# Softmax weights turned in 32x32 blocks on VectorE and multiplied by the values in sixteen 32x32 tiles, in a decoder layer in float32 on one core of Trainium2

## The chip, the cores and the metric

The kernel runs on one core of one Trainium2 chip. Its time is the device time of one execution in microseconds (us). Before the change it is 1048.2 us, the median of three runs (1045.29 to 1048.98). The engines are TensorE (PE in the profile, with its weight loads as PEld), VectorE (DVE), ScalarE (ACT), GpSimd (POOL) and SyncE (SP), which here only issues transfers.

## The reference: what is computed

One decoder layer with post-normalisation over x of 2 x 2048 rows of 512, all in float32: linear self-attention without softmax, cross-attention with 16 heads of 32 over 154 context rows, and a feed-forward part with token shift. Each ends in a residual sum and a layernorm.

```python
def _L0_xattn_ref(Query, Key, Values, Mask, ...):
    q = _split_heads(Query @ W_q.T + b_q)          # 16 heads of 32
    k = _split_heads(Key @ W_k.T + b_k)
    v = _split_heads(Values @ W_v.T + b_v)
    scores = jnp.einsum('bhqd,bhkd->bhqk', q, k) / jnp.sqrt(jnp.float32(D_K))
    scores = jnp.where(Mask == 0, jnp.float32(NEG_INF), scores)
    attn = jax.nn.softmax(scores, axis=-1)
    out = jnp.einsum('bhqk,bhkd->bhqd', attn, v)
    ...
    return out @ W_o.T + b_o
x = _layernorm(x + _L0_attn_ref(x, ...), axis=-1)
x = _layernorm(x + _L0_xattn_ref(x, ctx_1024, ctx_1024, mask, ...), axis=-1)
x = _layernorm(x + _L0_ffn_ref(x, ...), axis=-1)     # r = sigmoid(xr W_r), k = relu(xk W_k)^2, out = r * (k W_v)
```

## The kernel before, in words

There are three stages. `context_and_gram` (up to 97 us) loads x once and builds its Gram matrix, the keys and the values of the context. `fold` (to 188 us) folds the linear self-attention of each of the two batches into one matrix `m` and one row `c_row`. `layers` (the rest) runs the layer itself on 16 groups of 256 rows (two tiles of 128 rows, `t` = 0 and 1), 8 groups for each batch.

`layers` is a software pipeline that is written out by hand. The loop variable `n` is the group whose softmax runs; in the same pass group `a = n + 1` gets its self-attention product `y`, its layernorm, its turning (`x1_turn`) and its `q`; group `f = n - 1` gets the output product `o`, the second layernorm (`x2_turn`) and the mixing; group `e = n - 2` gets the products `k`, `r` and `v` of the feed-forward part. Each engine has its own program with its own order, and counts semaphores: `x.at(n, k)` is the count after k steps of group n. An engine runs its instructions in the order written, so a waiting instruction holds all behind it.

Each dense product is three float32r passes (`three_pass`, lines 81 to 83) over a high and a low part. Twelve such half products of 12 or 24 matmuls belong to one pass of the loop. They share two banks of PSUM, `d0` and `d1`.

The softmax of a group goes in four head groups `g` of 4 heads (32 partitions each in `q` and `kt`). For each: `scores` puts 8 products (2 tiles by 4 heads, 154 keys) into four banks; `masked_min` on VectorE adds the mask and takes the minimum of the negated scores, one instruction for each head; `exponentials` on ScalarE; `weigh` on GpSimd divides by the sum. The weights are then turned on TensorE (`transposes`): four 128x128 blocks for each tile (the first 128 keys), which ScalarE copies out (`take_turned`), and one block for each tile with the last 26 keys of the four heads, from a buffer of its own, `prob_rest` (`take_rest`). `values` multiplies: one 128x128 product for the 26 last keys of all heads and four 128x32 products for the first 128. `o_high` (ScalarE) and `o_low` (VectorE) split the result for the product `o`. A matmul on float32 data that is no transpose stands as two rows in the trace.

The names that the change and the prediction touch: `scores`, `transposes`, `values`, `masked_min`, `o_low`, `k_square`, `k_mix_low` (line 805), `v_finish` (lines 823 and 826, then `moments`), `normalise` (line 735), `weigh` (928 to 934).

## Time and profile before

| | |
|---|---|
| median of three runs | 1048.2 us (1045.29 to 1048.98) |
| the profiled execution | 1045.77 us, its span 1043.8 us |
| TensorE busy | 969.0 us, 6354 matmul rows and as many weight loads |
| VectorE busy | 648.7 us |
| ScalarE, GpSimd busy | 530.6 us, 527.3 us |
| one steady pass of the loop | 49.04 us |

The span is what the trace covers; the profiled execution took 2.0 us more than it. Busy time is a union of an engine's instructions, so a TensorE that reads 93% may still be waiting for nothing or be slowed within its rows: how far apart the starts of two rows are says more than their length. The steady pass is read from the first score row of one pass (602.58) to that of the next (651.62); the five passes from 553.55 to 798.73 are alike, at 49.03 to 49.04 us each.

### The profile page before, as it was taken

How to read it: one execution, taken by the hardware profiler on the slowest of the kernel's cores; microseconds unless marked ns; L12 is line 12 of the kernel's file. 1: busy time of each engine (PE TensorE's matmuls, PEld its weight loads, DVE VectorE, ACT ScalarE, POOL GpSimd, SP SyncE). 2: the span in 40 equal slices, each digit the busy share in tenths (PEclk: the TensorE clock that was granted, in tenths of full speed). 3: DMA queues.
4: the chain of work that ended last, by engine and by line, in shares of the span. 5: the costliest groups of instructions: out<-in, count | busy, mean ns of one | idle time of the engine just before them, and what ended most of it. 6: DMA issues, size and time to landing. Idle time of an engine off the chain costs nothing.

```text
span 1043.8 us, 18201 instructions
## 1 busy us (share of the span) xinstructions
PE 969.0 (93%) x6354; PEld 761.7 (73%) x6354; DVE 648.7 (62%) x1942; ACT 530.6 (51%) x1619; POOL 527.3 (51%) x525
## 2 busy tenths in 40 slices
PE   5999999667889999999999999999999999999875
PEld 4698474455677878878787878787877878787764
DVE  1243232245656867777778767777777677776753
ACT  1232022067565665656665656575756656565421
POOL 4283000147564756556657556474757566556310
PEclk9999999877989999999999999999999999999989
DMA  5253900100000101010110000000101010000001
GB/s 195 61 181 107 309 23 10 63 21 27 7 22 7 42 7 42 7 42 27 40 58 22 27 22 27 27 21 27 36 13 42 7 42 13 36 1 22 21 1 40
DMA packets 30853, 45.59 MB, mean 44 GB/s; under 512 B 2731, under 2 KB 15531, under 8 KB 30507
## 3 DMA queue, kind: packets, MB, share of 16 engines
q1 hardware_dynamic: 28363, 40.39, 11.9%
q10 hardware_dynamic: 2400, 4.05, 1.1%
q8 instruction: 51, 0.84, 0.3%
q14 instruction: 39, 0.32, 0.1%
HBM read 34.10 MB, written 9.70 MB: 42 GB/s over the span
## 4 chain that ended last, share of the span: by engine, by line
PE 66%; DVE 7%; issue 4%; ACT 3%; POOL 2%; DMA 1%; POOLq 0%; DVEq 0%
PE dense L81 18%; PE dense L83 16%; PE dense L82 16%; PE turned L1049 5%; PE scores L1039 3%; PE rest_value L1065 3%; PE rest_value L1062 3%; DVE mix_r_raw L799 2%; PE dense L999 1%; PE rest_value L1055 1%; DVE xt_lo L750 1%; ACT x_t L626 1%; ACT prob L584 1%; DVE prob L759 1%; DMA mask_in<-mask 1%
## 5 line engine op out<-in xcount | busy, mean ns | idle before, releaser
L928 POOL TENSOR_TENSOR row_inv<-row_sum,minus_one 128x4 f32<-128x4 f32 x128 | 143.1, 1118 | 187.8 <-ACT prob L584 187.8
L584 ACT ACTIVATE prob<-prob,row_min 128x154 f32<-128x154 f32 x512 | 209.8, 417 | 24.6 <-DVE row_min L759 24.5
L759 DVE CUSTOM_DVE_ANT_0 prob<-scores,mask_add 128x154 f32<-128x154 f32 x512 | 129.2, 310 | 44.2 <-PE scores L1039 44.2
L934 POOL TENSOR_TENSOR prob<-prob,row_inv 128x512 f32<-128x512 f32 x128 | 138.3, 1080 | 0.0
L592 ACT ACTIVATE prob_t<-turned 128x512 f32<-128x512 f32 x128 | 76.0, 594 | 102.9 <-PE turned L1049 102.9
L584 ACT ACTIVATION_READ_ACCUMULATOR prob<-prob,row_min 128x1 f32 x512 | 98.7, 193 | 0.0
L1049 PE MATMUL turned<-ident,prob 128*128 128x128 f32 x512 | 81.9, 284 | 8.5 <-POOL prob L934 4.6
L939 POOL TENSOR_TENSOR mix_r_lo<-mix_r_raw,mix_r_hi 128x1024 fp32r<-128x1024 f32 x16 | 38.2, 2390 | 100.3 <-ACT mix_r_hi L630 100.3
L81 PE MATMUL dense<-xt_hi,cross_wq_hi 128*128 128x256 f32 x256 | 78.2, 306 | 3.9 <-DVE xt_lo L750 3.9
L81 PE MATMUL dense<-mix_k_hi,ffn_wk_hi 128*128 128x256 f32 x256 | 74.3, 290 | 6.1 <-DVE xt_lo L750 4.4
L1049 PEld LDWEIGHTS turned<-ident,prob 128*128 128x128 f32 x512 | 60.0, 144 | 24.4 <-issue 10.7
L82 PE MATMUL dense<-xt_lo,cross_wq_hi 128*128 128x256 f32 x256 | 75.1, 293 | 0.0
L83 PE MATMUL dense<-xt_hi,cross_wq_lo 128*128 128x256 f32 x256 | 74.9, 293 | 0.0
L83 PE MATMUL dense<-mix_k_hi,ffn_wk_lo 128*128 128x256 f32 x256 | 71.4, 279 | 0.0
L82 PE MATMUL dense<-mix_k_lo,ffn_wk_hi 128*128 128x256 f32 x256 | 71.4, 279 | 0.0
L920 POOL TENSOR_TENSOR rstd<-var,neg_half 128x2 f32<-128x2 f32 x48 | 33.5, 698 | 74.2 <-DVE var L729 71.4
L173 POOL TENSOR_TENSOR x_sum<-x_sum,x_rows 128x512 f32<-128x512 f32 x32 | 48.0, 1500 | 36.6 <-DMA x_rows<-x_rows 32.6
L766 DVE TENSOR_TENSOR o_t_lo<-rest_value,o_t_hi 128x256 fp32r<-128x256 f32 x64 | 26.8, 419 | 62.2 <-ACT o_t_hi L603 62.2
L81 PE MATMUL dense<-ffn_wv_hi,k_act_hi 128*128 128x512 f32 x128 | 54.3, 424 | 8.3 <-DVE k_act_lo L817 8.3
L81 PEld LDWEIGHTS dense<-xt_hi,cross_wq_hi 128*128 128x128 f32 x256 | 51.8, 202 | 11.0 <-issue 6.2
L81 PEld LDWEIGHTS dense<-mix_k_hi,ffn_wk_hi 128*128 128x128 f32 x256 | 48.1, 188 | 15.5 <-issue 15.4
L81 PE MATMUL dense<-ffn_wr_hi,mix_r_hi 128*128 128x512 f32 x128 | 53.3, 416 | 3.8 <-ACT x_t L626 3.8
(143 smaller groups left out, 2653.0 us busy)
## 6 DMA issues: line engine op xcount, KB each, us to landing
x_rows<-x_rows SPq DMA_DIRECT2D x32, 256.0 KB, 2.8
xt_raw<-x_cols SPq DMA_DIRECT2D x16, 512.0 KB, 3.6
out<-gate_then_y SPq DMA_DIRECT2D x16, 512.0 KB, 2.8
mask_in<-mask SPq DMA_DIRECT2D x16, 154.0 KB, 2.3
w_v_raw<-cross_wv ACTq DMA_DIRECT2D x1, 1024.0 KB, 8.1
w_k_raw<-cross_wk ACTq DMA_DIRECT2D x1, 1024.0 KB, 10.8
self_wv<-self_wv ACTq DMA_DIRECT2D x1, 1024.0 KB, 5.2
self_wk<-self_wk SPq DMA_DIRECT2D x1, 1024.0 KB, 5.7
```

The source lines that it names most:

```text
L81: pe.matmul(out, sta[0], mov[0], start=first, stop=False, skip_group_check=True)
L82: pe.matmul(out, sta[0], mov[1], start=False, stop=False, skip_group_check=True)
L83: return pe.matmul(out, sta[1], mov[0], start=False, stop=last, skip_group_check=True)
L173: pool.tensor_tensor(x_sum[:, b, :], x_sum[:, b, :], x_in[t][:], ALU.add).then_inc(*summed.up)
L584: m = act.activation(keys, keys, ACT.Exp, bias=row_min[:, buf, t, h:h + 1], scale=-1.0, accum_out=row_sum[:, buf, t, h:h + 1])
L592: act.activation(pt[:, 0:HPG, t * P:(t + 1) * P], t_bank[:].rearrange("p (c n) -> p c n", c=HPG), ACT.Copy).then_inc(*t_out.up)
L759: m = dve.tensor_tensor_reduce(prob[buf][:, t, h * CTX:(h + 1) * CTX], s_bank[:, h, t * CTX:(t + 1) * CTX], mask_add[n % 2][:, t, :], -SCA ...
L920: pool.tensor_tensor(rs[:], var[:], neg_half[:], ALU.pow).then_inc(*ln_rstd[key].up)
L928: pool.tensor_tensor(row_inv[:, buf, t, :], row_sum[:, buf, t, :], minus_one[:], ALU.pow).then_inc(*p_inv.up)
L934: pool.tensor_tensor(keys[:, :, 0:P], keys[:, :, 0:P], inv.broadcast_to([P, HPG, P]), ALU.mult).then_inc(*p_norm.up)
L939: pool.tensor_tensor(mix["r"][1][:], mixed["r"][:], f32(mix["r"][0][:]), ALU.subtract).then_inc(*mix_lo["r"].up)
L1049: m = pe.transpose(t_bank[:, h * P:(h + 1) * P], prob[g % 2][:, t, h * CTX:h * CTX + P], ident[:])
```

## The change

Turning moves from TensorE to VectorE. For each tile and head group one instruction turns 640 columns (4 heads of 160, that is 154 keys padded to 5 blocks of 32) in blocks of 32x32, from `prob` into `prob_t`. In such a block the 32 keys lie on partitions, but each quarter of the partitions holds other rows of x, so `values` becomes 80 products of 32x32 stationary by 64 moving columns: 5 key blocks, 4 quarters of the partitions `i`, 4 heads. Quarter `i` writes to bank `i` of the four score banks, behind the scores. The values lie in SBUF four times over (`v_blocks`), are parked in DRAM and loaded for each batch (`load_values`). `transposes`, `take_turned`, `take_rest` and `prob_rest` are gone, and their two banks become dense banks: four in place of two, with other waits for a free bank. `scores` now waits until `o_low` has read the value part of the same banks (`ot_lo`), and `values` until `masked_min` has read the next scores (`s_min`). Two pieces move from VectorE to ScalarE: the layernorm's scaling (`normalise`, with a shift that GpSimd makes) and the square of the relu. Orders change with it: VectorE's `k_mix_low` now stands behind the minimum of the next group's first scores.

```diff
+def load_values(sp, v_blocks, v_park, b, flag):
+    first = v_park[b * CTX:b * CTX + 4 * DK, :].rearrange("(c j) d -> j c d", j=DK)
+    last = v_park[b * CTX + 4 * DK:(b + 1) * CTX, :]
+    for row in range(0, P, DK):
+        sp.dma_start(v_blocks[row:row + DK, 0:4, :], first).then_inc(*flag.up)
+        sp.dma_start(v_blocks[row:row + CTX - 4 * DK, 4, :], last).then_inc(*flag.up)
...
@@ layers, sp_program @@
+                if n and live(n) and n % GPB == 0:
+                    sp.wait_ge(*pv_mm.at(n - 1))
+                    load_values(sp, v_blocks, v_park, batch(n), v_here)
...
@@ layers, act_program @@
-            def take_turned(n, g, t):
-            def take_rest(n, g):
+            def normalise(key, n, rows):
+                _, _, _, _, rs, shift = norm[key]
+                act.wait_ge(*ln_shift[key].at(n))
+                for t in range(TPG):
+                    act.activation(rows[:, t, :], rows[:, t, :], ACT.Identity, bias=shift[:, t:t + 1],
+                                   scale=rs[:, t:t + 1]).then_inc(*ln_ok[key].up)
...
-                act.activation(relu[:, kt2, :], halves((d0, d1)[h]), ACT.Relu).then_inc(*k_relu.up)
+                act.activation(relu[:, kt2, :], halves(k_bank[h]), ACT.Relu).then_inc(*k_relu.up)
+                act.wait_ge(*k_relu.at(n, h + 1))
+                act.activation(square[:, kt2, :], relu[:, kt2, :], ACT.Square).then_inc(*k_sq.up)
...
@@ layers, dve_program @@
+            def turn_weights(n, g, t):
+                dve.wait_ge(*p_norm.at(n, g * TPG + t + 1))
+                if n + g:
+                    dve.wait_ge(*pv_mm.at(n, g))
+                dve.transpose(prob_t[:, t, :], prob[g % 2][:, t, :]).then_inc(*turned.up)
...
-            def k_square(n, h):
-            def normalise(key, n, rows):
...
@@ layers, pool_program @@
-                pool.tensor_tensor(after, keys[:, :, P:CTX], inv.broadcast_to([P, HPG, CTX - P]), ALU.mult)
-                pool.tensor_tensor(keys[:, :, 0:P], keys[:, :, 0:P], inv.broadcast_to([P, HPG, P]),
-                                   ALU.mult).then_inc(*p_norm.up)
+                pool.tensor_tensor(keys, keys, inv.broadcast_to([P, HPG, CTX]), ALU.mult).then_inc(*p_norm.up)
...
@@ layers, pe_program @@
             def scores(n, g):
                 pe.wait_ge(*q_out.at(n, g // 2 + 1))
+                if g:
+                    pe.wait_ge(*ot_lo_ok.at(n, g - 1))
+                elif n:
+                    pe.wait_ge(*ot_lo_ok.at(n - 1, HG - 1))
...
-            def transposes(n, g, t):
...
             def values(n, g):
-                pe.wait_ge(*t_out.at(n, (g + 1) * TPG))
-                pe.wait_ge(*rest_out.at(n, g + 1))
-                b = batch(n)
-                pe.matmul(value, v_rest[:, b, g, :], pt[:, HPG, :], start=True, stop=False, skip_group_check=True)
-                for h in range(HPG):
-                    cols = slice((g * HPG + h) * DK, (g * HPG + h + 1) * DK)
-                    m = pe.matmul(value[h * DK:(h + 1) * DK], v_first[:, b, cols], pt[:, h, :],
-                                  start=False, stop=True, skip_group_check=True)
+                pe.wait_ge(*turned.at(n, (g + 1) * TPG))
+                if n * HG + g + 1 < NG * HG:
+                    pe.wait_ge(*s_min.at(n, (g + 2) * TPG))
+                if n and n % GPB == 0 and g == 0:
+                    pe.wait_ge(*v_here.at(0))
+                for c in range(BLOCKS):
+                    for i in range(HPG):
+                        rows = slice(i * DK, (i + 1) * DK)
+                        for h in range(HPG):
+                            m = pe.matmul(value[h * DK:(h + 1) * DK, i, :],
+                                          v_blocks[rows, c, (g * HPG + h) * DK:(g * HPG + h + 1) * DK],
+                                          prob_t[rows, :, h * KEYS + c * DK:h * KEYS + (c + 1) * DK],
+                                          start=(c == 0), stop=(c == BLOCKS - 1), skip_group_check=True)
```

How the order moves. TensorE before, from the end of `y_product(a, 1)` to `r_product(e, 0)`: the four turns of tile 1 and the two of the rest stand between the two products (`turned` is the bank of the turned weights).

```order
L83 MATMUL dense<-m_hi,xt_lo 128x512
L1049 MATMUL turned<-ident,prob_1342 128x128 [waits t_out,p_norm]
L1049 MATMUL turned<-ident,prob_1342 128x128 x3
L1055 MATMUL rest_value<-ident,prob_rest_1344 128x128 [waits ot_lo]
L1055 MATMUL rest_value<-ident,prob_rest_1344 128x128
L81 MATMUL dense<-ffn_wr_hi,mix_r_hi 128x512 [waits y_sum,mix_lo_r]
L82 MATMUL dense<-ffn_wr_lo,mix_r_hi 128x512
```

TensorE at the same place now: the products follow each other.

```order
L92 MATMUL dense<-m_lo,xt_hi 128x512
L93 MATMUL dense<-m_hi,xt_lo 128x512
L91 MATMUL dense<-ffn_wr_hi,mix_r_hi 128x512 [waits o_sum,mix_lo_r]
L92 MATMUL dense<-ffn_wr_lo,mix_r_hi 128x512
L93 MATMUL dense<-ffn_wr_hi,mix_r_lo 128x512
```

Nothing stands between them any more. The next place is the head group's product with the values, between `r_product(e, 0)` and the turning of the second layernorm's rows (line 999 before, 983 now). Before:

```order
L83 MATMUL dense<-ffn_wr_hi,mix_r_lo 128x512
L1062 MATMUL rest_value<-prob_t,v_rest 128x256 [waits rest_out,t_out]
L1065 MATMUL rest_value<-prob_t,v_first 32x256 x4
L999 MATMUL dense<-ident,x_0_1368 128x128 [waits y_sum,ln2]
L999 MATMUL dense<-ident,x_0_1368 128x128 x3
L999 MATMUL dense<-ident,x_0_1368 128x128 [waits r_out,ln2]
L999 MATMUL dense<-ident,x_0_1368 128x128 x3
```

Now:

```order
L93 MATMUL dense<-ffn_wr_hi,mix_r_lo 128x512
L1051 MATMUL scores_values<-prob_t,v_blocks 32x64 [waits s_min,turned]
L1051 MATMUL scores_values<-prob_t,v_blocks 32x64 x79
L983 MATMUL dense<-ident,x_1_1373 128x128 [waits ln2]
L983 MATMUL dense<-ident,x_1_1373 128x128 x3
L983 MATMUL dense<-ident,x_1_1373 128x128 [waits y_sum,ln2]
L983 MATMUL dense<-ident,x_1_1373 128x128 x3
```

Five products have become 80, and they wait for `turned` and `s_min` in place of `t_out` and `rest_out`.

VectorE before, in front of the minimum of the next group's first scores (line 759, eight instructions for each tile, of which the first two are shown):

```order
L784 COPY x_t<-x_t 128x4 [waits mixed_ok_k,mixed_ok_r]
L766 TENSOR_TENSOR o_t_lo<-rest_value,o_t_hi 128x256 [waits ot_hi]
L817 TENSOR_TENSOR k_act_lo<-square,k_act_hi 128x512 [waits ka_hi]
L805 TENSOR_TENSOR mix_k_lo<-mix_k_raw,mix_k_hi 128x1024 [waits mix_hi_k]
L759 ISA prob_1341,row_min<-scores,mask_add_1347 128x154 [waits s_mm,mask_ok]
L759 ISA row_min 128x1
```

and from the last of these to the low part of the last head group's result (`o_low`, line 766):

```order
L759 ISA row_min 128x1
L823 SCALAR_TENSOR_TENSOR gate_then_y<-gate_then_y,dense 128x512 [waits v_mm,r_out]
L826 SCALAR_TENSOR_TENSOR gate_then_y<-gate_then_y,x_1_1369 128x512 [waits v_out]
L722 BN_STATS stats_1357<-gate_then_y 128x6 [waits v_sum]
L724 BN_AGGR moments_1358<-stats_1357 128x2 [waits stat3]
L823 SCALAR_TENSOR_TENSOR gate_then_y<-gate_then_y,dense 128x512 [waits v_mm,r_out]
L826 SCALAR_TENSOR_TENSOR gate_then_y<-gate_then_y,x_1_1369 128x512 [waits v_out]
L722 BN_STATS stats_1357<-gate_then_y 128x6 [waits v_sum]
L724 BN_AGGR moments_1358<-stats_1357 128x2 [waits stat3]
L729 TENSOR_SCALAR var_1359<-moments_1358 128x2 [waits rstd3,mom3]
L766 TENSOR_TENSOR o_t_lo<-rest_value,o_t_hi 128x256 [waits ot_hi]
```

VectorE now, at the same place (the minimum is line 745, `v_finish` lines 811 and 814, `moments` 712 to 720):

```order
L745 ISA row_min 128x1
L799 TENSOR_TENSOR mix_k_lo<-mix_k_raw,mix_k_hi 128x1024 [waits mix_hi_k]
L811 SCALAR_TENSOR_TENSOR gate_then_y<-gate_then_y,dense 128x512 [waits v_mm,r_out]
L814 SCALAR_TENSOR_TENSOR gate_then_y<-gate_then_y,x_1_1373 128x512 [waits v_out]
L712 BN_STATS stats_1359<-gate_then_y 128x6 [waits v_sum]
L714 BN_AGGR moments_1360<-stats_1359 128x2 [waits stat3]
L811 SCALAR_TENSOR_TENSOR gate_then_y<-gate_then_y,dense 128x512 [waits v_mm,r_out]
L814 SCALAR_TENSOR_TENSOR gate_then_y<-gate_then_y,x_1_1373 128x512 [waits v_out]
L712 BN_STATS stats_1359<-gate_then_y 128x6 [waits v_sum]
L714 BN_AGGR moments_1360<-stats_1359 128x2 [waits stat3]
L719 TENSOR_SCALAR var_1361<-moments_1360 128x2 [waits shift3,mom3]
L720 TENSOR_SCALAR minus_mean_1362<-moments_1360 128x2
```

The low part of the mix (128x1024) has moved from ahead of the minimum to between the minimum and `v_finish`, and a small instruction (`minus_mean`) is new; `o_low` (line 759 now) follows next.

## Rows read from the trace of the kernel before

**Rows 1.** The page: busy time of the engines, the granted clock in 40 slices, the chain
```profile
PE 969.0 (93%) x6354; PEld 761.7 (73%) x6354; DVE 648.7 (62%) x1942; ACT 530.6 (51%) x1619; POOL 527.3 (51%) x525
PEclk9999999877989999999999999999999999999989
PE 66%; DVE 7%; issue 4%; ACT 3%; POOL 2%; DMA 1%; POOLq 0%; DVEq 0%
```

**Rows 2.** Busy time by engine in one steady period (columns: the first row)
```profile
core 0: us, PE busy (x) PEld busy (x) DVE busy (x) ACT busy (x) POOL busy (x), PEclk, DMA share, GB/s
602.58:651.62 49.04, 48.44 (x353) 39.34 (x352) 36.64 (x115) 30.20 (x97) 29.73 (x31) 1.00 0.08 26
```

**Rows 3.** TensorE's timeline in that period: start us, length us, what, count
```profile
602.58 0.81 PE L1039 MATMUL scores<-kt,q 32*128 32x154 f32 x16
603.32 0.66 PE L1049 MATMUL turned<-ident,prob 128*128 128x128 f32 x4
603.73 0.48 PE L81 MATMUL dense<-cross_wo_hi,o_t_hi 128*128 128x512 f32 x1
604.05 0.39 PE L82 MATMUL dense<-cross_wo_lo,o_t_hi 128*128 128x512 f32 x1
...
606.34 0.40 PE L83 MATMUL dense<-cross_wo_hi,o_t_lo 128*128 128x512 f32 x1
606.58 0.60 PE L1049 MATMUL turned<-ident,prob 128*128 128x128 f32 x4
607.01 0.38 PE L1055 MATMUL rest_value<-ident,prob_rest 128*128 128x128 f32 x2
607.15 0.48 PE L81 MATMUL dense<-cross_wo_hi,o_t_hi 128*128 128x512 f32 x1
...
609.97 0.59 PE L1062 MATMUL rest_value<-prob_t,v_rest 128*128 128x256 f32 x2
610.49 0.64 PE L1065 MATMUL rest_value<-prob_t,v_first 128*32 128x256 f32 x8
611.06 0.50 PE L81 MATMUL dense<-m_hi,xt_hi 128*128 128x512 f32 x1
611.40 0.39 PE L82 MATMUL dense<-m_lo,xt_hi 128*128 128x512 f32 x1
```

**Rows 4.** The same, 610.480 to 610.515 (matmuls) and to 610.541 (weight loads)
```profile
610.49 0.42 PE L1065 MATMUL rest_value<-prob_t,v_first 128*32 128x256 f32 x4
610.49 0.16 PEld L1065 LDWEIGHTS rest_value<-prob_t,v_first 128*32 128x32 f32 x8 [0.33 <-issue]
```

**Rows 5.** The two waits of TensorE in that period, in brackets, from its timeline
```profile
623.87 0.50 PE L81 MATMUL dense<-ffn_wr_hi,mix_r_hi 128*128 128x512 f32 x1 [0.26 <-ACT x_t L626]
...
629.47 0.36 PE L81 MATMUL dense<-mix_k_hi,ffn_wk_hi 128*128 128x256 f32 x1 [0.34 <-DVE xt_lo L750]
```

**Rows 6.** VectorE's groups over five periods: busy us, mean ns of one | idle before
```profile
L759 DVE CUSTOM_DVE_ANT_0 prob<-scores,mask_add 128x154 f32<-128x154 f32 x160 | 40.4, 310 | 11.5 <-PE scores L1039 11.5
L805 DVE TENSOR_TENSOR mix_k_lo<-mix_k_raw,mix_k_hi 128x1024 fp32r<-128x1024 f32 x5 | 16.9, 3389 | 0.0
L735 DVE TENSOR_SCALAR x<-x,moments,rstd 128x512 f32<-128x512 f32 x20 | 10.0, 544 | 4.1 <-POOL rstd L920 4.1
L766 DVE TENSOR_TENSOR o_t_lo<-rest_value,o_t_hi 128x256 fp32r<-128x256 f32 x20 | 8.4, 418 | 13.0 <-ACT o_t_hi L603 13.0
L743 DVE TENSOR_TENSOR x<-dense,c_row 128x512 f32<-128x512 f32 x10 | 6.8, 684 | 0.0
L724 DVE BATCH_NORM_AGGREGATE moments<-stats 128x2 f32<-128x6 f32 x30 | 5.5, 182 | 1.0
```

**Rows 7.** DMA queue of TensorE's instructions: packets, MB, share of 16 engines
```profile
q8 instruction: 51, 0.84, 0.3%
```

**Rows 8.** GpSimd's weighing of the first 128 keys, from the page
```profile
L934 POOL TENSOR_TENSOR prob<-prob,row_inv 128x512 f32<-128x512 f32 x128 | 138.3, 1080 | 0.0
```

**Rows 9.** A transfer of 256 KB from SyncE: count, KB each, us to landing
```profile
x_rows<-x_rows SPq DMA_DIRECT2D x32, 256.0 KB, 2.8
```

More of the change, by code:

```diff
@@ L17 @@
 HG = HEADS // HPG
-GK = HPG * CTX
+BLOCKS = -(-CTX // DK)
+KEYS = BLOCKS * DK
 SELF_DH = 64
@@ L458, in layers @@
     bq = col_sb[:, 2 * KT:3 * KT]
-    s_bank, t_bank, rv_bank, d0, d1 = psum
-    rest_t, value = rv_bank[:, 0:GT], rv_bank[:, GT:2 * GT]
+    sv_bank, dense = psum
+    bank_of = lambda first, second: (dense[first], dense[second])
+    k_bank, o_bank, y_bank, r_bank = bank_of(0, 3), bank_of(1, 2), bank_of(3, 0), bank_of(1, 0)
+    x2t_bank, x1t_bank, q_bank, v_bank = bank_of(2, 3), bank_of(1, 2), bank_of(0, 1), bank_of(2, 3)
+    value = sv_bank[:, :, TPG * CTX:TPG * CTX + TPG * DK]
+    tokens = lambda rows: rows.rearrange("p (t q i) -> p q t i", t=TPG, q=HPG)
+    value_out = value.rearrange("p q (t i) -> p q t i", t=TPG)
     live = lambda n: 0 <= n < NG
@@ L946, in add_bias @@
                                    ALU.add).then_inc(*x1_bo.up)
-            for t in rest:
+            for t in prob:
                 pool.memset(t[:], 0.0).then_inc(*setup.up)
@@ L1252, in decoder_layer @@
         behind_gram = mem.at
-        placements = context_and_gram(nc, io, mem, kv, x_ring, v_raw, x_sum, col_sb, gram, fold_w)
+        context_and_gram(nc, io, mem, kv, x_ring, v_raw, x_sum, col_sb, gram, fold_w)
         mem.at = behind_gram
-        fold(nc, io, mem, x_sum, col_sb, gram, banks, fold_w, m[1:], c_row, weights, xt, placements,
-             (m_park, c_park, parked), late_in)
+        fold(nc, io, mem, kv, v_raw, x_sum, col_sb, gram, banks, fold_w, m[1:], weights, xt, park, late_in)
     with ExitStack() as ctx:
-        psum = [ctx.enter_context(nc.psum_tensor(name, shape, F32)) for name, shape in
-                (("scores", [P, HPG, D]), ("turned", [P, D]), ("rest_value", [P, D]), ("dense0", [P, D]),
-                 ("dense1", [P, D]))]
+        psum = (ctx.enter_context(nc.psum_tensor("scores_values", [P, HPG, D], F32)),
+                [ctx.enter_context(nc.psum_tensor(f"dense{i}", [P, D], F32)) for i in range(4)])
         mem.at = main_at
-        layers(nc, io, mem, kv, col_sb, psum, weights, m, xt, (m_park, c_park, parked), late_in, out)
+        layers(nc, io, mem, kv, col_sb, psum, weights, m, xt, park, late_in, out)
 def kernel(**inputs):
```

345 lines of the change are left out of this document (140 added, 205 removed).

## The prediction

> **What bounds the kernel now.** I read the page first. TensorE is busy for 93% of the span and the chain that ended last runs 66% through it, with 7% on VectorE [rows 1]. Busy time alone does not show that TensorE is full, so I took one steady pass, 49.04 us: TensorE is busy for 48.44 us of it at a granted clock of 1.00, VectorE for 36.64, ScalarE and GpSimd for some 30 each [rows 2]. In its timeline the starts follow each other without a hole except for two short waits, 0.26 us for the turned x2 and 0.34 us for the low part of x1 [rows 5]. So a pass is TensorE's own work plus 0.60 us, and what leaves TensorE shortens it until another engine's chain is longer. The reader should see two more things. The turns of tile 0 take from 603.32 to 603.73 and the dense product behind them begins with a step of 0.32 us where 0.24 is usual (606.34 to 606.58); the turns of tile 1 with the rest take from 606.58 to 607.15; the product with the values takes from 609.97 to 611.06 [rows 3].
>
> **What TensorE loses.** 0.41 + 0.57 us, and 0.08 us twice for the slower first step behind them: 1.15 us for a head group, some 4.5 us for the four of a pass (one of the eight turns stands behind another turn and is cheaper) [rows 3]. The 0.60 us of waits [rows 5] hung on the two dense banks (the second `r_product` waited for `x2t_out`, `k_product(e, 1)` for `x1t_lo`); with four banks both conditions are gone or older, so I take them off too.
>
> **What TensorE gets.** 80 products of 32x32 by 64 columns. A float32 product is two rows here, and a row of 256 columns costs 0.213 us (in the 128x128 product with `v_rest`, whose two rows and the switch behind them take 0.52 us: 2 x 0.213 + 0.09) [rows 3]. So a 64-column row costs 0.053 us in its tile, ten rows for each of 16 tiles: 0.53 us if the tiles ran fully side by side. They can't: each needs a start of its own. Where the array is cut in four, four matmuls have started within 23 ns and eight weight loads within 50 ns [rows 4], one pair each 6.7 ns. I take this pace for all 160 pairs: 1.07 us. Add 0.09 us to enter the other tiling, 0.05 us for the last columns and 0.09 us to leave it: 1.30 us where 1.09 was, so +0.21 us, +0.85 us a pass. Nothing in the trace shows this pace over more than a handful of pairs. The bounds: 0.53 + 0.23 = 0.76 us from below, and from above the pace of the scores, 16 pairs in 0.74 us [rows 3], 46 ns a pair, or 7.6 us; there the 154 columns set the pace and not the starts, so I stay at the near end. TensorE's pass becomes 49.04 - 4.5 - 0.6 + 0.85 = 44.8 us.
>
> The supply of instructions was looked at too. 0.84 MB for 12708 rows are 66 bytes each; 51 packets took 0.3% of 16 engines' span, 1.0 us for 250 instructions, 7.9 ns a pair [rows 1, 7]. If nothing were fetched ahead, a head group would take 1.5 us in place of 1.3, 0.8 us a pass, less than the slack found below.
>
> **VectorE.** It gets eight block transposes of 128x640 a pass. No such row exists. From below: the scaling in SBUF takes 544 ns for 512 columns, 0.68 us for 640. From above: the 128x1024 difference takes 3389 ns, 2.1 us for 640. The ordinary rows, 418 ns for 256 columns and 684 for 512, give 1.04 ns a column and 0.82 us for 640; a one-input copy is nearest to them, and I take 0.8 us [rows 6]. The Trainium skill ("VectorE: DVE Perf Modes", The three transpose paths) gives 311 ns for a bf16 block transpose of 128x128. The slope above would give 285 ns, so rule and row go together, and by the page a row of 640 would be some 0.84 us by the same slope. VectorE also gets three small instructions of 0.2 us, and loses six scalings (3.3 us) and two squares of 0.69 us (like the 128x512 rows) [rows 6]: 36.6 + 6.4 + 0.6 - 3.3 - 1.4 = 38.9 us of a 44.8 us pass. It isn't full, but it works in order, and one stretch is too long. `scores(n + 1, 1)` now waits for `o_low` of the head group before it, and that stands behind all this, counted from the end of `scores(a, 0)`: minimum 1.0 (four heads at 40.4 / 160 us), transpose 0.8, minimum 1.0, `k_mix_low` 3.4 (moved into this stretch), `v_finish` of tile 0 with three 128x512 rows and one small 2.25, of tile 1 2.6, `o_low` 0.4 us: 11.45 us [rows 6]. TensorE has two halves of `v_product` (12 steps of 0.23 and one slow start, 2.85 us each), values 1.3 and half of `k_product` 2.85 us to do meanwhile, 9.85 us [rows 3]. So TensorE waits 1.6 to 1.7 us there once a pass, and a pass is 46.5 us. The same wait covers the 0.8 us that instruction supply may cost only if it falls in this stretch; I leave it out.
>
> **ScalarE and GpSimd** are costed at nothing. ScalarE loses eight copies of 128x512 and four of 128x256 and gets six scalings and two squares of 128x512. GpSimd loses the instruction for the last 26 keys, and the other grows from 512 to 616 columns, 1.08 to 1.30 us [rows 8]. Both stay near 30 us of 46, which hides them; behind a late `v_finish` the scaling of y3 now stands ahead of the relu of `k` on ScalarE, which VectorE's `k_low` waits for. What hides it is the wait for `o_product` behind `k_low`; if that cover is gone it costs tenths of a us a pass.
>
> **SyncE.** In `fold` the parking and the eight loads take the place of eleven small transfers, ahead of weights that are not needed before `layers`: nothing. At group 8 the values of the second batch are loaded in eight transfers between the last product of group 7 and the first of group 8: `k_product`, `scores`, two halves of `o_product`, 9.4 us. A transfer of 256 KB lands in 2.8 us [rows 9]: overlapped, hidden; one after the other 22 us, a wait of 13 us once. I take 0; the far end goes into the range.
>
> **The sum.** 49.04 - 46.5 = 2.5 us a pass. Sixteen groups, of which the first and the last run at a lower clock or among other waits: 15 passes, 38 us. The profiled execution took 1045.8 us, 2.4 below the median; I take the 38 us off the median: **1010 us**.
>
> **The rivals.**
>
> *The pace of the small pairs does not hold* (slower, 18%). For it: no row has more than 16 pairs in a burst, and 160 follow here. Against it: loads and matmuls keep the same pace side by side. It decides from the point where the pass is 49.04 again: 1.30 + 4.24 / 4 = 2.36 us a head group, 13.3 ns a pair, twice the pace of rows 4. At 16 ns a pass takes 50.8 us and the kernel 1048 + 26 = 1075 us; at the scores' 46 ns a pass takes 70 us and the kernel some 1360 us. The Trainium skill ("TensorE: Matmul & The Clock Gate", Wait — 56ns, not 53.3ns?) says that starts never come closer than about 25 ns, however few columns. By that alone a group would take 4.2 us and the kernel some 1160 us. The rows contradict it for different tiles: 6.7 ns [rows 4].
>
> *The transpose costs two passes over its columns* (about no change, 15%). At 1.6 us each VectorE has 45.3 us of work in a pass, and the long stretch grows by 0.8 us; with its in-order waits I get 48.5 to 49.5 us a pass, 1040 to 1055 us. For it: nothing shows float32 through a transposing path. Against it: the slope.
>
> *VectorE's long stretch is hidden* (15%), because `k_mix_low` no longer meets GpSimd's work and takes 1.2 us (the 1.04 ns a column above) in place of 3.4: then a pass is 44.8 us, and the kernel 1048 - 64 = 984 us.
>
> *Other new waits* (6%), each of the bank conditions being new: 1025 to 1055 us.
>
> *The likeliest* (46%): 995 to 1030 us, at 1010.
>
> **How the numbers follow.** All of the first 46% and 15% are faster, 5 of the 15 of the dear transpose and 4 of the last 6: 70%. A change within 0.5%, which is about what these runs can tell from none: 6 + 1 + 1 = 8%. Slower: 17 + 4 + 1 = 22%. The range goes from 982 us, the hidden stretch, to 1075 us, the pace at 16 ns; the far end of the loads' wait, 13 us, lies inside; some 6% lie below and 11% above.
>
> **What would show it.** The new `values` rows: start of the first to start of the dense product behind them 1.2 us, and clock 1.00. STREAM_TRANSPOSE rows of 0.8 us. A pass of 46.5 us with one wait of TensorE, at line 1037 for `o_low`, of about 1.6 us. Wrong I am if the 160 pairs take over 2.4 us, if VectorE's rows of 640 columns are over 1.5 us, or if TensorE waits at `values` itself, which would mean that exponentials, weighing and turning are late.

## The result and the profile after

The changed kernel takes 1074.99 us (median of 4 runs, 1071.48 to 1077.08) where the kernel before takes 1048.07: 1.026 times as long, interval 1.022 to 1.029. It is slower by 27 us. The prediction said 38 us faster.

The page of the changed kernel, with the lines that answer to [rows 1, 7] and two groups that are new:

```profile
PE 963.9 (90%) x15314; PEld 783.0 (73%) x15314; DVE 659.7 (62%) x1990; ACT 536.8 (50%) x1555; POOL 514.7 (48%) x445
...
PEclk9998999766889999999998999999899999999987
...
q8 instruction: 120, 1.97, 0.8%
...
L1051 PE MATMUL scores_values<-prob_t,v_blocks 32*32 32x64 f32 x10240 | 120.7, 229 | 43.1 <-issue 25.0
L755 DVE STREAM_TRANSPOSE prob_t<-prob 128x640 f32<-128x640 f32 x128 | 103.5, 828 | 10.3 <-POOL prob L919 10.3
```

TensorE has 15314 matmul rows where it had 6354, and its clock dips in the middle of the kernel, which it did not before. TensorE sat idle for 43.1 us ahead of rows of the values, 25.0 us of it with "issue" as the releaser, which means that the profile names nothing that it waited for. In the windows below the first two rows are passes without a long stall, the third is a pass with one, the last the whole steady stretch (columns as in [rows 2]):

```profile
704.90:752.01 47.11, 47.11 (x913) 39.72 (x912) 37.04 (x118) 30.56 (x93) 27.52 (x25) 1.00 0.09 28
...
854.17:901.18 47.01, 47.01 (x914) 39.66 (x913) 37.07 (x118) 30.56 (x93) 28.91 (x26) 1.00 0.09 29
...
752.01:803.63 51.62, 49.80 (x914) 42.22 (x913) 36.65 (x118) 30.68 (x94) 28.80 (x26) 0.93 0.08 26
...
353.41:954.01 600.60, 579.91 (x10945) 488.66 (x10944) 447.22 (x1417) 368.40 (x1117) 346.17 (x302) 0.97 0.10 31
```

An undisturbed pass takes 47.0 to 47.1 us, 2.0 less than the 49.04 of [rows 2]: the gain is there. But twelve passes take 600.6 us, 50.05 each. In TensorE's timeline an undisturbed group of values and a disturbed one look like this:

```profile
896.25 1.78 PE L1051 MATMUL scores_values<-prob_t,v_blocks 32*32 32x64 f32 x160
897.96 0.39 PE L91 MATMUL dense<-xt_hi,cross_wq_hi 128*128 128x256 f32 x1
```

```profile
505.70 1.72 PE L1051 MATMUL scores_values<-prob_t,v_blocks 32*32 32x64 f32 x152
509.24 0.44 PE L1051 MATMUL scores_values<-prob_t,v_blocks 32*32 32x64 f32 x8 [1.82 <-issue]
509.61 0.58 PE L91 MATMUL dense<-mix_k_hi,ffn_wk_hi 128*128 128x256 f32 x1
...
510.42 0.41 PE L91 MATMUL dense<-mix_k_hi,ffn_wk_hi 128*128 128x256 f32 x1
510.63 0.41 PE L92 MATMUL dense<-mix_k_lo,ffn_wk_hi 128*128 128x256 f32 x1
...
512.34 0.31 PE L91 MATMUL dense<-mix_k_hi,ffn_wk_hi 128*128 128x256 f32 x1
512.49 0.28 PE L92 MATMUL dense<-mix_k_lo,ffn_wk_hi 128*128 128x256 f32 x1
```

The first goes from 896.25 to 897.96, 1.71 us from its first start to the next product's. The second stops after 152 of its 160 rows, 2.04 us from start to start, with no releaser, and the 256-column products behind it step by 0.21 us until 512.34, where 0.12 is usual: the granted clock from 509.24 to 512.34 is 0.50, the lower level, 1.2 GHz, after 1.82 us of idleness. Such a stall is paid twice: the pass from 752.01 is 4.6 us longer than an undisturbed one, 2.0 us by its stall and most of the rest by the lower clock. Shorter stalls can pass without that: in the pass from 353.41, with steps of 1.21 and 0.61 us, the clock is 1.00.

Where the time went, by lining up the end of each of the 64 groups of values (four to a pass, counted from 0) with its twin before. Spans of the profiled executions: 1069.4 against 1043.8. The first row counts from the start of the span. The first scores stand at 208.45 here and at 212.09 before, so from the first scores to group 8 the loss is 13.9 us. Those 3.6 us ahead of the scores are not shown to be the change's: e6_ramp, whose program is the same up to there, has its first scores at 212.30.

| stretch | change |
|---|---|
| up to group 8 | +10.2 us |
| groups 8 to 59 | +9.2 us: 51 groups at -0.51 is -26; 22 us of stalls inside groups; the rest (13) is the clock behind them, edges behind groups, 1 to 2 us at the change of batch |
| behind group 59 | +6.1 us |

**The regularity.** I counted TensorE's recorded instructions (matmul rows, weight loads, semaphore instructions) from the start of the trace. From 326 to 960 us there are 18 steps of over 0.48 us between matmul starts. Fourteen of them fall at the same count, 193 or 194 above a multiple of 256. Of the other four one is the change of batch (558.15, two further on) and three lie between two products at the low clock. A packet of the instruction queue is 16 KB, 120 of them for some 30900 instructions, so it holds 256. I call that place an edge. For the stalled group at 505.70 the records say: previous edge passed at 505.81, transfer of the next packet from 506.92 to 507.89, TensorE goes on at 509.24. In 13 of the 14 steps of over 0.9 us at an edge from 320 to 990 us TensorE goes on 1.3 to 1.6 us after the packet has landed and 2.4 to 3.9 us after it passed the edge before (the fourteenth is the change of batch, where VectorE's minima are waited for). A group of values issues 320 instructions, so it can meet two edges, 256 instructions and undisturbed some 1.2 to 1.4 us apart.

### The profile page after: what moved, and what is told of

It reads as the page before. It is cut to its first block, busy times and chain, and to the rows that moved or that the text cites. A ratio compares the mean times of both kernels' runs of the same rounds, so it can differ in the third digit from the quotient of the medians.

```text
span 1069.4 us, 35864 instructions
## 1 busy us (share of the span) xinstructions
PE 963.9 (90%) x15314; PEld 783.0 (73%) x15314; DVE 659.7 (62%) x1990; ACT 536.8 (50%) x1555; POOL 514.7 (48%) x445
## 4 chain that ended last, share of the span: by engine, by line
PE 70%; DVE 4%; issue 4%; ACT 2%; POOL 2%; DMA 1%; ACTq 0%; DVEq 0%; POOLq 0%
PE dense L91 19%; PE dense L93 17%; PE dense L92 17%; PE scores_values L1051 10%; PE scores_values L1037 4%; PE dense L983 3%; DVE prob L745 1%; ACT prob L590 1%; POOL prob L919 1%; DVE mix_k_raw L793 1%; POOL row_inv L916 1%; DMA mask_in<-mask 1%; DVE stats L712 0%; POOL rstd L907 0%; DVE prob_t L755 0%
## 5 line engine op out<-in xcount | busy, mean ns | idle before, releaser
L745 DVE CUSTOM_DVE_ANT_0 prob<-scores_values,mask_add 128x154 f32<-128x154 f32 x512 | 128.6, 312 | 63.9 <-PE scores_values L1037 63.6
L919 POOL TENSOR_TENSOR prob<-prob,row_inv 128x616 f32<-128x616 f32 x128 | 161.4, 1261 | 10.0
L1051 PE MATMUL scores_values<-prob_t,v_blocks 32*32 32x64 f32 x10240 | 120.7, 229 | 43.1 <-issue 25.0
L1051 PEld LDWEIGHTS scores_values<-prob_t,v_blocks 32*32 32x32 f32 x10240 | 104.7, 104 | 63.8 <-issue 59.4
L755 DVE STREAM_TRANSPOSE prob_t<-prob 128x640 f32<-128x640 f32 x128 | 103.5, 828 | 10.3 <-POOL prob L919 10.3
L605 ACT ACTIVATE o_t_hi<-scores_values 128x256 fp32r<-128x256 f32 x64 | 24.6, 385 | 137.2 <-PE scores_values L1051 137.2
L759 DVE TENSOR_TENSOR o_t_lo<-scores_values,o_t_hi 128x256 fp32r<-128x256 f32 x64 | 27.0, 421 | 96.9 <-ACT o_t_hi L605 96.8
L91 PE MATMUL dense<-mix_k_hi,ffn_wk_hi 128*128 128x256 f32 x256 | 77.8, 304 | 0.0
L92 PE MATMUL dense<-mix_k_lo,ffn_wk_hi 128*128 128x256 f32 x256 | 75.1, 293 | 0.3 <-issue 0.3
L598 ACT ACTIVATE x<-x,shift,rstd 128x512 f32<-128x512 f32 x64 | 48.5, 806 | 32.4 <-POOL shift L909 32.3
L91 PE MATMUL dense<-ffn_wv_hi,k_act_hi 128*128 128x512 f32 x128 | 55.3, 432 | 10.2 <-DVE k_act_lo L805 10.2
## 6 DMA issues: line engine op xcount, KB each, us to landing
w_k_raw<-cross_wk ACTq DMA_DIRECT2D x1, 1024.0 KB, 11.5
```

Of the source, the lines that this page charges most:

```text
L91: pe.matmul(out, sta[0], mov[0], start=first, stop=False, skip_group_check=True)
L92: pe.matmul(out, sta[0], mov[1], start=False, stop=False, skip_group_check=True)
L598: act.activation(rows[:, t, :], rows[:, t, :], ACT.Identity, bias=shift[:, t:t + 1], scale=rs[:, t:t + 1]).then_inc(*ln_ok[key].up)
L745: m = dve.tensor_tensor_reduce(prob[buf][:, t, h * KEYS:h * KEYS + CTX], sv_bank[:, h, t * CTX:(t + 1) * CTX], mask_add[n % 2][:, t, :], - ...
L755: dve.transpose(prob_t[:, t, :], prob[g % 2][:, t, :]).then_inc(*turned.up)
L919: pool.tensor_tensor(keys, keys, inv.broadcast_to([P, HPG, CTX]), ALU.mult).then_inc(*p_norm.up)
```

## The experiments

Theory 1: TensorE's instructions arrive too late where two edges lie less than some 3.3 us apart (e4_shift shows that this takes one more condition). Theory 2: the small products themselves or a clash with other work stretch the groups. The columns "start", "middle" and "end" are the change against the kernel before up to group 8, to group 59 and behind, in us, from each profiled execution. "From scores" is the start counted from the first scores; the time ahead of them differs by up to 3.8 us between profiled executions of kernels that are the same up to there, so it is the better column. Each ratio is to the kernel before in the same series of runs, whose median was 1048.07 up to e4, 1048.71 for e5 to e7 and 1050.44 for e8 and e9.

| kernel | median us | ratio to before | start | from scores | middle | end |
|---|---|---|---|---|---|---|
| changed | 1074.99 | 1.026 (1.022 to 1.029) | +10.2 | +13.9 | +9.2 | +6.1 |
| e1_split | 1086.12 | 1.035 (1.032 to 1.039) | +11.5 | +15.1 | +14.3 | +11.7 |
| e2_four_blocks | 1016.24 | 0.970 (0.966 to 0.973) | +6.9 | +7.7 | -39.4 | +0.6 |
| e3_half_columns | 1066.6 (one run) | | +14.0 | +14.2 | +1.7 | +5.2 |
| e4_shift | 1051.61 | 1.004 (1.001 to 1.006) | +10.4 | +9.5 | -9.1 | +3.6 |
| e5_steer | 1046.51 | 0.998 (0.997 to 1.000) | +11.1 | +12.0 | -18.2 | +6.5 |
| e6_ramp | 1069.91 | 1.020 (1.017 to 1.023) | +11.0 | +10.8 | +8.3 | +1.2 |
| e7_both | 1044.15 | 0.996 (0.994 to 0.997) | +10.1 | +10.9 | -19.7 | +7.2 |
| e8_steer_all | 1040.67 | 0.993 (0.990 to 0.995) | +12.1 | +10.4 | -19.7 | +2.8 |
| e9_late_split | 1037.47 | 0.990 (0.987 to 0.992) | +7.1 | +7.1 | -18.8 | +0.2 |

**e1_split.** The group in two parts, the first one dense step earlier:

```diff
                 if live(f):
                     o_product(f, 0)
+                if live(n):
+                    values(n, 0, 0, CUT)
+                if live(f):
                     o_product(f, 1)
                 if live(n):
-                    values(n, 0)
+                    values(n, 0, CUT, BLOCKS)
```

`CUT` is 3; the other three groups of a pass are split in the same way.

> The 80 products of each group of values are issued in two parts, key blocks 0 to 2 (48 products) one dense step of 12 products earlier than now, and blocks 3 and 4 (32 products) at the old place, so that 12 dense products (1.3 to 2.7 us) lie between the parts; the work is the same. Theory 1 (instruction supply): a product in four-byte floats is four instructions, a group is 320, and the instruction queue brings 16 KB, which is 256 instructions, at a time; a group stalls when two of these edges are passed within less time than the queue needs for a block, some 3.3 us. With the dense products between, two edges are at least 2.7 to 4 us apart: the 14 groups that now take 2.7 to 4.7 us fall to no more than 0.5 us of stall each, the granted clock in the steady stretch rises from 0.97 to 0.99 or more, a pass takes 47.0 plus 4 times 0.25 us for the second entry and exit, 48.0, and the kernel takes some 1036 us (1028 to 1045). Theory 2 (the small products themselves, or a clash with other engines over the memories, cause the long groups): as many products run beside the same work, the long groups stay and the time is 1075 us or, with the second entries, up to 1090.

From 354 to 960 us no step over 0.48 us falls at an edge: the first parts take 1.08 to 1.10 us, the second 0.78, and the clock from 354 to 945 us is 0.99. Theory 1 has its groups. The time is wrong by 50 us, by my placement. The first part came too early for the row minima of the next group's scores, which `values` waits for. The waits in the steady stretch of this kernel:

```profile
PE scores_values L1053 <- DVE row_min L746: 16.6, 24, 4.9
PE scores_values L1053 <- DMA v_blocks<-v_scratch: 1.5, 1, 1.5
```

The second entry and exit add 0.25 us, four times a pass. Together they cost the middle 5 us more than the stalls had (+14.3 against +9.2).

**e2_four_blocks.** 64 products a group; keys 128 to 153 are left out.

```diff
-                for c in range(BLOCKS):
+                for c in range(BLOCKS - 1):
...
-                                          start=(c == 0), stop=(c == BLOCKS - 1), skip_group_check=True)
+                                          start=(c == 0), stop=(c == BLOCKS - 2), skip_group_check=True)
```

> The fifth key block (keys 128 to 153 of each head) is left out of the values, so that part of the attention is missing; 64 products, 256 instructions, to a group. Theory 1 (instruction supply): a group can no longer hold two edges of 256 instructions, so the stalls inside groups, 40 us in sum now, fall to a few us; the undisturbed group falls from 1.72 to 1.39 us, and with the clock back near 1.00 the kernel takes some 1010 us (1000 to 1025). Theory 2 (a cost that goes with the number of products): the excess falls by a fifth, 40 to 32 us, the groups by 0.33 times 64, 21 us, and the kernel takes 1046 us.

The group takes 1.40 us, no step is over 0.55 us in the steady stretch but the change of batch (2.5 us), and an undisturbed pass takes 45.7 us. The kernel is 59 us faster than the changed one for a fifth of the products: 0.32 x 64 = 20 us of it is the products' own, and the rest is most of all what 256 instructions do not meet and 320 do. Theory 1 had 1010 us (1000 to 1025), theory 2 had 1046.

**e3_half_columns.** As many instructions, half of the columns in blocks 1 to 4; the second token tile lacks them.

```diff
-    m = pe.matmul(value[h * DK:(h + 1) * DK, i, :], ...
-                  prob_t[rows, :, ...
+    took = slice(0, TPG * DK if c == 0 else DK)
+    m = pe.matmul(value[h * DK:(h + 1) * DK, i, took], ...
+                  prob_t[rows, 0:(TPG if c == 0 else 1), ...
```

> Key blocks 1 to 4 are multiplied for the first of the two token tiles alone (32 moving columns in place of 64), so that half of these sums is missing; there are as many products and instructions as before. On the undisturbed pace of 10.2 ns an instruction pair: if a band of 32 rows passes 64 moving and 32 weight columns of each of its pairs one after the other (96 columns at 2.4 GHz, 40 ns, four bands beside each other, 10 ns), the later blocks fall to 64 columns, 6.7 ns a pair, and the group from 1.72 to 1.29 us; if the pace is one of issuing instructions, it stays at 1.71 us. On the stalls: theory 1 (instruction supply) keeps them, in the same groups, at 1.5 to 2.5 us each or somewhat more, since as many instructions pass in less time; theory 2 (work or memory traffic of the products) takes a good part of them away. Time by theory 1 with the columns: about 1050 us.

The stalls stay, 23 us inside the groups from 8 to 59 as against 22, and of the twelve groups over 2 us eleven are the same (8, 18, 23, 28, 32, 37, 38, 43, 48, 57 and 58). So the stalls hang neither on the work nor on the traffic of the products. On the pace both readings fell: from the 33rd pair on, the starts come every 9.0 ns on average, neither 6.7 nor 10.2, and the undisturbed group takes 1.53 us. The time, 1066.6, misses my 1050 with it.

**e4_shift.** 128 instructions ahead of all groups (`SHIFT` is 32):

```diff
             def y_product(n, t):
+                if n + t == 0:
+                    for _ in range(SHIFT):
+                        pe.matmul(y_bank[0][0:DK, 0:DK], ident[0:DK, 0:DK], ident[0:DK, 0:DK], start=True, stop=True,
+                                  skip_group_check=True)
```

> 32 products of 32x32 on the unit matrix (128 instructions, about 1 us) are issued once, ahead of the first product with the folded weights, into a bank that the next product overwrites; nothing else changes. Theory 1 (instruction supply): the stalls lie where an edge of 256 instructions falls 36 to 65 instructions after a group's first, with the next one inside or just behind the same group. In the changed kernel that is groups 8, 18, 23, 28, 37, 38, 43, 48, 57, 58 and 61 (counted from 0 in order of time, four to a pass). Shifted by 128 the edges fall there in groups 40, 60 and, at 66 and 67, 25 and 26: these become long, the eleven become undisturbed at 1.72 us, and the time falls by some 20 to 35 us, to 1040 to 1057. Theory 2 (anything tied to a place in the program, such as a clash with a store, a load or VectorE): the same groups stay long and the time stays at 1075 us or 1 us more.

The stalls moved where the count said. Group 23 (stalled at 505.70 above) is whole, and group 25, undisturbed before, stalls right behind its last row; TensorE's timeline of this kernel:

```profile
503.59 1.79 PE L1056 MATMUL scores_values<-prob_t,v_blocks 32*32 32x64 f32 x160
505.31 0.38 PE L92 MATMUL dense<-mix_k_hi,ffn_wk_hi 128*128 128x256 f32 x1
```

```profile
526.06 1.79 PE L1056 MATMUL scores_values<-prob_t,v_blocks 32*32 32x64 f32 x160
530.66 0.69 PE L984 MATMUL dense<-ident,x 128*128 128x128 f32 x3 [2.81 <-issue]
```

Groups 25, 26 and 60, which I had named, take 4.60, 3.86 and 3.56 us, and the eleven that I had named as freed take 1.72 each. The miss is group 40, which stayed whole. 23 us came back for one microsecond of useless products. All steps of over 0.7 us from 355 to 956 us, eight of them, fall at 193 or 194 above a multiple of 256. The two kernels together give the stall by the number of instructions from a group's first to the next edge (us above the usual step, at the edge after that one):

```
instructions to the edge   8-36    37-42     47-64     65-75     80-92     97-240
stall, us                  0-0.3   0.7-1.6   2.0-2.9   1.0-2.1   0.1-1.1   0 to 0.5
```

Seven instructions gave one stall of 1.5, and at 243 to 248 there are 0.2 to 0.4 us at the first edge.

The column 8-36 does not fit theory 1 as I put it: from 320 to 1000 us the two kernels have 13 pairs of edges only 1.2 to 1.4 us apart without a stall. The packets tell why. In these 13 pairs the transfer of the packet that the second edge needs began 1.0 to 2.4 us ahead of the first edge; in the 20 stalls of over 0.9 us (the change of batch apart) it began from 0.2 us ahead of that edge to 2.0 us behind it, and TensorE went on 1.2 to 1.6 us after it had landed. So a stall takes two edges close together and a packet whose transfer did not begin early. What makes it begin early in one place and not in another is not shown.

**e5_steer.** With that table the edges can be kept out of the bad places by 48 useless products (the expectation counts 58; its list adds up to 48):

```diff
+FILL = {6: 9, 14: 6, 20: 3, 25: 2, 30: 9, 36: 2, 41: 3, 46: 9, 52: 2, 57: 3}
...
+                for k in range(FILL.get(n * HG + g, 0)):
+                    rows = slice(k % HPG * DK, (k % HPG + 1) * DK)
+                    pe.matmul(sv_bank[rows, k % HPG, 0:DK], ident[rows, rows], ident[rows, rows], start=True, stop=True,
+                              skip_group_check=True)
```

> 58 products of 32x32 on the unit matrix (232 instructions in the whole kernel, some 1 to 2 us) are issued in ten places ahead of scores, into columns that these scores overwrite: 9, 6, 3, 2, 9, 2, 3, 9, 2 and 3 of them ahead of the scores 6, 14, 20, 25, 30, 36, 41, 46, 52 and 57 (counted from 0, four to a pass). They are chosen so that no edge of 256 instructions falls 36 to 96 instructions after the first of a group of values, where the traces of the changed kernel and of the shifted one show stalls of 0.4 to 2.9 us, while outside it there are none over 0.4 us. The work is otherwise that of the changed kernel. Theory 1 (instruction supply): no gap over 0.6 us in TensorE's stream between groups 8 and 60 but the wait for VectorE at the change of batch; the granted clock of that stretch rises from 0.97 to 0.99 or 1.00; its passes take 47.0 to 47.3 us against 49.04 before, so that the 10.4 us lost there become 24 to 27 gained. The start and the end of the passes keep their loss of 10 and 3 us. Time 1036 us (1030 to 1043). Theory 3 (the instruction supply is only part, and other waits of the changed order take up what is freed): gaps of another kind appear and the time stays above 1045 us.

28 us faster than the changed kernel by more instructions and the same work. The middle went from +9.2 to -18.2 us, not to -24: four steps of 0.5 to 1.3 us at edges stayed. The start did not move, the end kept its 6.5 us (group 63 stalls at 65 instructions by the count of the table), and the time misses the expected range by 3.5 us.

**e6_ramp.** In the first pass VectorE takes the minima of group 1 ahead of turning group 0. The changed kernel, TensorE and VectorE at the first values:

```profile
211.58 1.07 PE L1037 MATMUL scores_values<-kt,q 32*128 32x154 f32 x16 [2.32 <-DVE row_min L745]
219.81 0.50 PE L1051 MATMUL scores_values<-prob_t,v_blocks 32*32 32x64 f32 x28 [7.16 <-DVE row_min L745]
```

```profile
216.93 0.84 DVE L755 STREAM_TRANSPOSE prob_t<-prob 128x640 f32<-128x640 f32 x1 [1.41 <-POOL prob L919]
217.70 0.28 DVE L745 CUSTOM_DVE_ANT_0 prob<-scores_values,mask_add 128x154 f32<-128x154 f32 x1
```

```diff
+                if n == 0:
+                    masked_min(n, 1, 0)
+                    masked_min(n, 1, 1)
                 if live(n):
                     turn_weights(n, 0, 0)
                     turn_weights(n, 0, 1)
+                if live(n) and n:
                     masked_min(n, 1, 0)
                     masked_min(n, 1, 1)
```

> In the first pass alone VectorE takes the row minima of the scores of group 1 ahead of turning the weights of group 0; nothing else changes. In the changed kernel the first values wait 7.6 us, the last of it for these minima (they end at 219.66, the turned weights were there at 217.78), and the softmax of group 1 starts only then. If the order on VectorE is what costs the start some 9 us, the first values start about 1.9 us earlier, the second group's weights are ready some 5 us earlier, and the kernel gains 3 to 8 us, to 1067 to 1072 us. If the start is bound by the chain of ScalarE and GpSimd or by the splitting of the weights on VectorE, the 1.9 us are given back at the next wait, and the time stays within 1.5 us of 1075. The stalls of the instruction supply should stay in their groups.

The same place in this kernel:

```profile
215.43 0.81 PE L1041 MATMUL scores_values<-kt,q 32*128 32x154 f32 x16 [2.32 <-DVE row_min L745]
221.69 1.56 PE L1055 MATMUL scores_values<-prob_t,v_blocks 32*32 32x64 f32 x101 [5.45 <-DVE prob_t L755]
```

6.3 us from the scores to the values in place of 8.2, as expected. The median is 5 us lower, inside the expected range. From the first scores to group 8 the profiled execution loses 10.8 us in place of 13.9, and e7_both 10.9 in place of the 12.0 of e5_steer, so 1 to 3 us are the start's. The rest of the gain lies at the end of the profiled execution (+1.2 against +6.1), which this edit does not explain.

**e7_both.**

> Both edits together. If they act in different places, the sum: 1036 less 3 to 8 us, 1030 us (1024 to 1037), 1.0 to 2.3 per cent faster than before. If the start gives nothing, 1036 us. If the instruction supply is not what holds the passes, above 1045 us.

1044.15 us, 0.4% faster than before, and 2.4 us under e5_steer: the two add up to less than I said, and the time lies outside the expected 1024 to 1037.

**e8_steer_all and e9_late_split.** The first has a new table, `FILL = {0: 32, 4: 15, 8: 12, 9: 12, 14: 8, 20: 3, 25: 3, 30: 8, 36: 3, 41: 3, 46: 8, 52: 3, 57: 3, 63: 9}`. These are 122 products, 74 more than in e5_steer, where the expectation says 60. The second also moves `weight_low(1)` of the first pass behind `masked_min(n, 3, 1)`.

> The two edits of the last kernel (the small products that steer the edges, and the minima of group 1 ahead in the first pass), with the table of small products made for the first eight groups and the last one too: 32, 15, 12, 12, 8, 3, 3, 8, 3, 3, 8, 3, 3 and 9 of them ahead of the scores 0, 4, 8, 9, 14, 20, 25, 30, 36, 41, 46, 52, 57 and 63. In the last kernel the groups 0, 5, 7 and 63 still stall by 1.6, 1.9, 2.5 and 2.2 us, at 47, 29, 214 and 67 instructions from their start to the next edge; behind a wait of some us the stalled places seem to be others than in a dense stretch, so the rule for the first groups is a guess from nine cases. Theory 1 (instruction supply): three or four of these four stalls go, at a price of about 1 us for 60 more small products; 1039 us (1036 to 1043). If at the start the queue is slow for another reason, two or more stay or appear elsewhere, and the time stays at 1044.

> The kernel before this one in the list, and in the first pass alone VectorE splits the second of the late weights (2.25 us) behind the low parts of the first pass's turned rows in place of ahead of them. In the changed kernel TensorE waits 3.9 us at 244.81 for these low parts, with a split of 2.3 us ahead of them on VectorE. If that order holds the start, a further 1.5 to 2.3 us go (1037 us); if the chain through the scores and the minima holds it, 0 to 0.5 us.

e8: the stalls of 1.6, 1.9 and 2.2 us in groups 0, 5 and 63 are gone, the end falls from +7.2 to +2.8, and the time lies in the expected range. But at the start group 1 now stalls for 2.35 us and group 7 still for 2.3, and from the first scores only 0.5 us are won. My rule for the first groups was no rule. e9 takes 3 us more off. TensorE's wait for the low part of x1 in the first pass, in the changed kernel and in e9:

```profile
244.81 0.58 PE L91 MATMUL dense<-xt_hi,cross_wq_hi 128*128 128x256 f32 x1 [3.48 <-DVE xt_lo L734]
```

```profile
243.63 0.39 PE L92 MATMUL dense<-xt_hi,cross_wq_hi 128*128 128x256 f32 x1 [1.41 <-DVE xt_lo L735]
```

2.1 us, as expected. A pass of e9 with the small products in it, and its steady stretch, whose clock is back at 1.00 (the row from 354 to 945 us of the changed kernel says 0.97):

```profile
875.74:922.81 47.07, 47.07 (x919) 39.78 (x919) 37.16 (x118) 30.55 (x94) 28.74 (x26) 1.00 0.08 25
```

```profile
354.00:945.00 591.00, 584.53 (x11443) 492.97 (x11442) 465.46 (x1462) 378.16 (x1151) 356.86 (x313) 1.00 0.10 31
```

e9 is the fastest kernel here that does all of the work: 1037.47 us, 1.0% under the kernel before, 3.5% under the changed one.

## Why the prediction was wrong

**The step that failed** is the paragraph on the supply of instructions. It priced a packet at its transfer, 1.0 us for 250 instructions, and spread it evenly: 7.9 ns a pair, at most 0.8 us a pass, hidden. The transfer was right (0.9 to 1.5 us). But a packet's transfer begins, at the median, only 1.0 us after its edge has been passed (23 of the 120 begin ahead of it), and the packet counts only 1.3 to 1.6 us after it has landed. So what matters is the time between two edges, with the lead that the packet has, and not the mean. Kernel before: an edge each 17 us or so, none under 13 us behind the last, none felt. Changed kernel: two edges inside one group, or one in it and one just behind, wherever it starts in the wrong place. In the middle stretch that is a fixed property of the program: e3_half_columns, with the same instructions, stalls in the same groups, about a quarter of all. e2 (no two edges in a group), e3 (same instructions, less work), e4 (same work, other places) and e5 (edges steered) each show it. Price: 22 us inside the groups of the middle stretch and some 35 with the clock behind them, edges behind groups and the change of batch; e5's 27 us in that stretch is the measured part.

The measured 1074.99 us lies at the far end of the stated range, 1075 us. That end was the price of a uniform pace of 16 ns a pair, which no run shows, so it is luck that the two agree.

**The second step that failed** is "sixteen groups, of which the first and the last run at a lower clock or among other waits", costed at no loss. From the first scores to group 8 the start loses 14 us, and the end 6. In the first passes there is little dense work to lay beside the softmax, and its chain now ends on VectorE. From 205 to 330 us TensorE waits 15.8 us at `values` for minima that VectorE takes only after turning, and 8.4 us for the low part of x1, where the kernel before waits 13.9 us for turned or weighed weights and 2.5 us for that low part. The granted clock there falls with the idleness: 0.67, 0.79 and 0.93 in the first three passes where the kernel before has 0.75, 0.85 and 1.00. The wait of 7.2 us at the very first values costs little by itself: they begin 11.4 us after the first scores, where they began 11.0 us after them before. Two queue orders give back 2 us each at their own waits (e6, e9). The rest of the start, +7 us in e9, is not taken apart.

**What TensorE loses**, 4.5 us a pass, and the 0.60 us of waits of [rows 5]: right as far as the sum shows. With the group at its measured length the working gives 44.8 + 4 x 0.51 = 46.8 us, and undisturbed passes take 47.0 to 47.1, TensorE busy throughout.

**The values** were mis-sized: 1.71 us from start to start where 1.2 was forecast, since the pace of [rows 4], 6.7 ns, holds for the first 32 pairs alone (180 ns, even a little faster) and the rest start every 10.2 ns on average. That alone leaves the kernel faster by some 30 us. The rival "the pace does not hold" named the right group and a threshold of 2.36 us. With its stalls the middle groups average 2.11 us, and the clock makes up the difference. But its mechanism, a uniform slower pace, is not what happened. The 25 ns from the Trainium skill ("TensorE: Matmul & The Clock Gate", Wait — 56ns, not 53.3ns?) does not hold across tiles: 160 starts in 1.57 us.

**VectorE**: the turn takes 0.83 us, as sized, and the rival of a double price is out. The wait of 1.6 us at the scores did not come in the steady passes, where `o_low` ends some 9 to 15 us ahead of the scores that wait for it. It came in the first and last passes, which the working left out: the scores at 238.02, 264.45 and 974.89 begin 0.10 us after `o_low` has ended, behind steps of 3.4, 1.3 and 1.5 us. The profile has "issue" as the releaser here too, so that word alone does not mean a late packet:

```profile
238.02 1.41 PE L1037 MATMUL scores_values<-kt,q 32*128 32x154 f32 x16 [3.15 <-issue]
```

```profile
237.49 0.43 DVE L759 TENSOR_TENSOR o_t_lo<-scores_values,o_t_hi 128x256 fp32r<-128x256 f32 x1 [2.53 <-ACT o_t_hi L605]
```

The rival that hides the long stretch had it right: `mix_k_lo` takes 1.24 us in its new place where [rows 6] had 3.4, in the pass from 854.17, beside the turns of that pass:

```profile
L755 DVE STREAM_TRANSPOSE prob_t<-prob 128x640 f32<-128x640 f32 x8 | 6.5, 826 | 0.2 <-POOL prob L919 0.2
...
L799 DVE TENSOR_TENSOR mix_k_lo<-mix_k_raw,mix_k_hi 128x1024 fp32r<-128x1024 f32 x1 | 1.2, 1240 | 0.0
```

Its reason is borne out too, by the trace of the kernel before. There `mix_k_lo` takes 3.39 to 3.40 us in the 13 passes where GpSimd's sum of 128x1024 (L945) runs beside it for 2.31 us, 1.59 us where that sum runs beside it for 0.51, and 1.23 us at 1006.51, where GpSimd does nothing. In the changed kernel the sum is beside it for at most 0.16 us:

```profile
343.98 3.39 DVE L805 TENSOR_TENSOR mix_k_lo<-mix_k_raw,mix_k_hi 128x1024 fp32r<-128x1024 f32 x1
```

```profile
343.47 2.82 POOL L945 TENSOR_TENSOR x<-x,cross_bo_row 128x1024 f32<-128x1024 f32 x1
```

**ScalarE, GpSimd, SyncE at nothing**: right in the steady passes (in groups 36 to 60 the weights are turned 3.5 to 9.7 us before their products; group 32, the first of the new batch, waits for no load).

Open: what sets 10.2 and 9.0 ns; what lets some packets begin early; why stalls at the start follow another rule.

## What to carry to other kernels

Count an engine's instructions before cutting work into small pieces: many short instructions in one burst have a cost that no mean of queue traffic shows, and it depends on where in the program the burst starts. Look for idle time with no releaser that comes back at one instruction count, then try a harmless shift of the stream. If it does not come back at one count, look for a semaphore wait that the profile has not named, as at the scores here. And cost the first and last passes of a pipeline by themselves: a chain that dense work hides in the middle is bare there.

## What the hardware showed that I had not expected

TensorE's instructions came in 16 KB packets of 256 throughout the run (120 here, 51 before). A packet was of use 1.3 to 1.6 us after landing. The Trainium skill ("Runtime: NRT & Kernel Launch", Instruction fetch mechanics) has an engine's instructions refilled in blocks of 16 KiB, 256 instructions, while it runs, at a cost that is mostly hidden. The trace agrees on the block, and on the cost in the kernel before; here 22 us of stalls in the middle stretch were not hidden. A float32 product of 32x32 tiles is four instructions, and pairs on 16 tiles start about each 6 ns for the first 32, then on average each 10.2 ns with 64 columns and 9.0 with 32. A VectorE row of 1.2 us took 3.4 us while GpSimd summed 128x1024 elements beside it. And 48 useless products made the kernel 28 us faster.
